# Second-layer output tiles placed behind three products instead of two in the group loop of a fused MLP and adapter kernel

## The reference

```python
attn_out = softmax(x Wq (x Wk)^T * scale) (x Wv) @ Wp + bp
cms_out  = gelu(attn_out @ cW1 + cb1) @ cW2 + cb2 + one_hot(codes)
modifier = gelu(concat[attn_out, cms_out] @ mW1 + mb1) @ mW2 + mb2
x        = clip(x + cms_out + modifier, 0, 1)
h        = x + gelu(x @ W_down[stream] + b_down) @ W_up[stream] + b_up
out      = layernorm(h) * ln_w[stream] + ln_b[stream]
```

## Time and profile before

| | |
|---|---|
| median of 3 runs | 1073.81 us (1073.79 to 1074.4) |
| time of the profiled execution | 1073.88 us |
| its span | 1072.0 us |
| PE busy | 1063.9 us (99%), 4753 instructions |
| PEld busy | 881.3 us (82%) |
| DVE busy | 598.1 us (56%) |
| POOL busy | 542.0 us (51%) |
| ACT busy | 452.6 us (42%) |
| granted clock of PE | full in all 40 slices |

### The profile page before, as it was taken

How to read it: one execution, slowest core, us unless ns; L and a number is a source line. 1 busy time by engine, 2 the same in 40 slices (tenths; PEclk the granted TensorE clock), 3 DMA queues, 4 the chain that set the end, 5 groups by cost and what they waited for, 6 DMA issues and landing times.

```text
span 1072.0 us, 13168 instructions
## 1 busy us (share of the span) xinstructions
PE 1063.9 (99%) x4753; PEld 881.3 (82%) x4753; DVE 598.1 (56%) x838; ACT 452.6 (42%) x868; POOL 542.0 (51%) x555
## 2 busy tenths in 40 slices
PE   9999999999999999999999999999999999999997
PEld 8888888888888888888888888888878888888886
DVE  4735344395565565566774445555885445545568
ACT  4624336353343333333454333343644433342664
POOL 0501154542243232332798667666997667753406
PEclk9999999999999999999999999999999999999999
DMA  7401010101223213112132221223934221123834
GB/s 276 139 1 40 1 40 20 40 0 45 74 73 123 100 73 108 36 34 65 60 109 84 84 84 66 83 84 140 354 121 167 84 79 55 64 69 147 294 79 157
DMA packets 62063, 100.50 MB, mean 94 GB/s; under 512 B 5680, under 2 KB 35376, under 8 KB 61488
## 3 DMA queue, kind: packets, MB, share of 16 engines
q1 hardware_dynamic: 61424, 98.62, 26.8%
q10 hardware_dynamic: 576, 1.05, 0.3%
HBM read 77.63 MB, written 22.02 MB: 93 GB/s over the span
## 4 chain that ended last, share of the span: by engine, by line
PE 92%; DVE 4%; POOL 3%; issue 1%; ACT 1%; DVEq 0%; ACTq 0%; POOLq 0%
PE bank L736 30%; PE bank L738 30%; PE bank L737 30%; DVE z L1522 1%; DVE stats L1516 1%; PE bank L793 1%; DVE c_T_f L1321 1%; POOL c_B_lo L568 1%; POOL left_c L568 0%; POOL left_x L568 0%; PE bank L762 0%; POOL c_T_lo L568 0%; DVE H_lo L1369 0%; DVE mean_var L1518 0%; POOL W_lo L568 0%
## 5 line engine op out<-in xcount | busy, mean ns | idle before, releaser
L1398 DVE TENSOR_TENSOR acc<-bank,acc 128x512 f32<-128x512 f32 x224 | 151.4, 687 | 88.9 <-PE bank L738 88.2
L736 PE MATMUL bank<-H_hi,W_hi 128*128 128x512 f32 x512 | 199.3, 389 | 0.7 <-POOL W_lo L568 0.7
L737 PE MATMUL bank<-H_lo,W_hi 128*128 128x512 f32 x512 | 199.2, 389 | 0.0
L738 PE MATMUL bank<-H_hi,W_lo 128*128 128x512 f32 x512 | 199.2, 389 | 0.0
L568 POOL TENSOR_TENSOR left_x<-rawX,left_x 128x256 fp32r<-128x256 f32 x144 | 126.8, 881 | 99.7 <-ACT left_x L992 99.7
L992 ACT ACTIVATE left_x<-rawX 128x256 fp32r<-128x256 f32 x144 | 58.0, 410 | 167.9 <-DMA rawX<-mW_dram 86.2
L1381 DVE TENSOR_TENSOR u_t<-bank,s_t 128x512 f32<-128x512 f32 x64 | 44.2, 690 | 131.8 <-PE bank L738 125.1
L736 PEld LDWEIGHTS bank<-H_hi,W_hi 128*128 128x128 f32 x512 | 96.1, 188 | 21.0 <-POOL W_lo L568 1.2
L738 PEld LDWEIGHTS bank<-H_hi,W_lo 128*128 128x128 f32 x512 | 96.1, 188 | 20.1
L737 PEld LDWEIGHTS bank<-H_lo,W_hi 128*128 128x128 f32 x512 | 96.1, 188 | 19.9
L736 PE MATMUL bank<-x_T_hi,left_x 128*128 128x512 f32 x256 | 99.6, 389 | 0.0
(11 more groups left out here) (195 smaller groups left out, 2309.0 us busy)
## 6 DMA issues: line engine op xcount, KB each, us to landing
rawX<-mW_dram SPq DMA_DIRECT2D x16, 512.0 KB, 3.9
rawC<-mW_dram SPq DMA_DIRECT2D x16, 512.0 KB, 5.0
W_raw<-mW_dram SPq DMA_DIRECT2D x16, 512.0 KB, 3.7
xT_raw<-xT_dram SPq DMA_DIRECT2D x4, 1024.0 KB, 8.3
x_raw<-x_dram SPq DMA_DIRECT2D x4, 1024.0 KB, 6.1
rawX<-cW_dram SPq DMA_DIRECT2D x8, 512.0 KB, 3.8
W_raw<-cW_dram SPq DMA_DIRECT2D x8, 512.0 KB, 3.7
out_dram<-z SPq DMA_DIRECT2D x16, 256.0 KB, 2.0
```

The lines of the kernel that those rows point to most:

```text
L736: pe.matmul(tile, sh, mh, start=first_one and n == 0, stop=False, skip_group_check=joined_group)
L737: pe.matmul(tile, sh, ml, start=False, stop=False, skip_group_check=joined_group)
L738: last = pe.matmul(tile, sl, mh, start=False, stop=last_one and n == len(terms) - 1, skip_group_check=joined_group)
L1398: op = dve.tensor_tensor(dst, src, dst, ALU.add)
```

## The change

A function `first_of` gives the number of products that PE issues before the first four output tiles: 2 in groups 17 and 24, 3 in all others. Group 16 leaves the loop before it is used, and group 0 has no output tiles, so the order changes in groups 1 to 15, 18 to 23 and 25 to 31, 28 groups in all. In these product 2 now stands ahead of `out_tiles(g - 1, 0)`, and was behind it. The second four output tiles stay behind product 4. No instruction is added or removed on any engine, and the orders of DVE, ACT, POOL and SP are the same.

```diff
+            def first_of(g):
+                return 2 if g in (MOD0 + 1, 24) else 3
...
                 else:
-                    for i in order_of(g)[g == 0:2]:
+                    for i in order_of(g)[g == 0:first_of(g)]:
                         product_part(g, i, sources)
                 if g > 0:
                     out_tiles(g - 1, 0)
-                for i in order_of(g)[2:5]:
+                for i in order_of(g)[first_of(g):5]:
                     product_part(g, i, sources)
                 if g > 0:
                     out_tiles(g - 1, 1)
```

## The result

| | median | lowest to highest | runs |
|---|---|---|---|
| before | 1074.06 us | 1073.57 to 1074.74 | 9 |
| changed | 1076.92 us | 1076.3 to 1078.45 | 9 |

The ratio is 1.003, with a 95% interval from 1.0019 to 1.004: slower by 2.86 us. That is 0.27%; the interval begins at 0.19%, just under the 0.2% that the prediction called the limit of a measurement. The forecast was 1074.5 us, no change, with a range up to 1075.8. The profiled execution took 1076.82 us, 2.94 more than that of before.

A forecast was written before the change was run, and what follows sets the result against it. PE was taken as the bound, so only its waits count. Group 1's 1.76 us less group 25's 1.03 gives +0.73 on 1073.88, 1074.61; with the median 0.07 below, 1074.5 us, range 1073.3 to 1075.8.

The forecast's parts named there:

- What bounds the kernel: Whole kernel: PE, busy 1063.9 of 1072.0 us and 92% of the chain; only its waits can change the time.
- The cms groups 2 to 14 and the modifier groups: Product 2's operands are ready with at least 1.34 us to spare in cms groups, 4.55 in modifier group 21: cost nothing.
- Group 1, 1.76 us: Group 1: PE newly waits for T1 from DVE, 1.63 us late plus 0.13 for slower steps.
- Group 25, 1.03 us gained: Group 25: product 2 covers PE's wait for `W_lo`, recovering 0.90 us and 0.13 for slower steps.
- The output tiles, later by a product: Group 15: DVE's last additions come 1.36 us later, delaying ACT and POOL; taken as 0, at worst 1.16 us.
- the upper bound of 1.16: Group 15's worst case: all 1.36 us of delay arrive, less 0.33 spare, plus 0.13 for slower steps.
- Rival 2: POOL's queue of groups 15 to 17 arrives late at 558.37: 1075.2 us, or 1075.7 with all the delay; chance 0.14.
- Rival 1: The clock falls once in group 1 during PE's new idle time: 1076.4 us, over 0.2% slower; chance 0.04.
- Rivals 3 and 4: Group 25's wait stays, 1075.6 us, chance 0.05; group 1 costs nothing, T1 being ready earlier, 1072.8 us, chance 0.03.

The follow-up runs named there:

- `not1`: The changed kernel with group 1 back at two products ahead of the output tiles: 1075.24 us, ratio 1.0013 against the kernel before.
- `t1_first`: The changed kernel with DVE writing the low half of T1 in group 1 ahead of two rows of its own: 1075.27 us, ratio 1.0012.
- `only25`: The kernel before with three products ahead of the output tiles in group 25 alone: 1073.65 us, ratio 0.9995.
- `sp_swap`: The changed kernel with SP's load of the next adapter piece in group 16 moved behind the eight cms saves: 1077.16 us, ratio 1.0029.
- `saves_first`: The changed kernel with SP issuing group 16's first four cms saves ahead of the loads of `rawX` and the piece: 1077.65 us, ratio 1.0029, four runs.
- `only15`: The kernel before with three products ahead of the output tiles in group 15 alone: 1076.85 us, ratio 1.0026.
- `only25_26`: The kernel before with three products ahead of the output tiles in groups 25 and 26: 1072.98 us, ratio 0.999.

## Why the prediction was right or wrong

The forecast of 1074.5 us was 2.4 us too low, and the time lies outside the range. Two terms of its sum came true; a third, put at nothing, did not.

**What bounds the kernel:** right. PE's share of the chain is 95% after, and each loss over 0.2 us was PE waiting for another engine's row.

**The cms groups 2 to 14 and the modifier groups:** right. None of those that moved lost more than 0.02 us. Group 24, which did not move, lost 0.15 us more than before; no run was made on it.

**Group 1, 1.76 us:** right, 1.81 lost, at 222.83 where 222.59 was forecast (the kernel began 0.15 us later). `not1` took it away and `t1_first` showed that two DVE rows made it.

**Group 25, 1.03 us gained:** right in size, 1.04. The sum took it as belonging to one place. Group 26's move may have been needed too (`only25`, not shown for certain); the change had both.

**"The output tiles, later by a product", group 15, taken as 0:** this is the step that failed. It cost 2.0 to 2.8 us between medians, beyond the upper bound of 1.16 as well. Its own reason was right: POOL's rows met less of DVE, and were only 0.7 us late. But the 0.49 us for which POOL waited for ACT before 538.56 were counted as spare, and I did not ask what ACT waited for. In the kernel before, ACT waited 0.23 us for the save of `cms_kept`. So that wait had no room at all. Between DVE's last addition and this save lies SP's queue, where a load stood ahead that was itself late (mending that alone gave back 0.5 of 1.8 us, `sp_swap`), and the DMA engines, where the load of `rawX` held the saves (`saves_first`). The step left both out. It also weighed the overlap with DVE for the two `rawX` rows only. The prediction's own sentence, that the delay could move POOL onto another of DVE's rows and block it anew, is what happened at 542.80, on the row right behind them, and made that row 0.75 us longer. Its upper bound took 1.36 us of delay to arrive as 1.36 at most, but ACT's row came 2.3 us later against PE.

One reading ahead of the step was wrong too: the prediction took the list of waits to mean that PE waited nowhere else inside the stream. The kernel before lost 0.13 us in group 16, at a matmul at 541.93, too little for the list. DVE's row on `c_T_lo` had ended 0.15 us ahead of it (540.01 + 1.77 = 541.78), which is about as far as PE started behind its releaser in group 1. So this stretch seems to have had no room in a second place as well.

**Rival 2** named the right work, POOL's rows of groups 15 to 17, and the wrong place: 558.37. The loss came at 544.34 first. Its own place did show, in `only15` and `saves_first`.

**Rival 1**, the clock, fell. PE was idle for 1.55 us before 222.83, and the granted clock of the windows around it, the third value from the end (the DMA share and GB/s follow), is 1.00:

```profile
216.00:224.00 8.00, 6.45 (x29) 5.03 (x28) 7.87 (x11) 7.58 (x12) 0.03 (x1) 1.00 0.00 0
224.00:230.00 6.00, 6.00 (x28) 4.94 (x28) 5.51 (x7) 1.67 (x3) 5.41 (x4) 1.00 0.00 0
```

PE stayed at its upper level of 2.4 GHz. The Trainium skill, TensorE: Matmul & The Clock Gate, section "A second HAM failure mode: psum-queue depth-cycling", would have allowed for a fall; this single idle time did not make one. The rival's price, 1.86 us, is not shown by a row either: in the kernel before the granted clock is 1.00 in each of the first six microseconds, so the slow transposes of the earlier trace rows are no measure of the lower level.

**Rivals 3 and 4** fell: `W_lo` was ready 1.76 us before its output tile, and T1 was no earlier than its row said.

## What to carry to other kernels

Before an operation of a full stream is moved, read at each place what its waits have to spare, and follow every queue behind what is made later, the DMA issue queue too: an engine that waits for another is not spare time until it is known what that other one waited for. The repeated groups of a steady stage took the new order for nothing; the first group, and the last before a change of stage, paid. A wait that goes can come back one group later when what was late hangs on a transfer, and may do so in some executions only, so a gain is to be followed for as many groups as the pattern repeats, and over more than one execution.

## What the runs showed of the hardware

- Four saves of 256 KB landed at most 3.1 us after the last tile's sum with the load of `rawX` (512 KB) issued behind them, 3.4 with it issued 3.3 us ahead of that sum (kernel before), and 4.7 to 5.2 us with it issued 2.3 us ahead.
- One load of 1024 KB took 5.7, 5.9 and 7.1 us from issue to landing in three executions (kernel before, `only25_26`, `only25`).
- One DVE instruction with two SBUF inputs (128x512) took 0.68 us alone and up to 2.65 beside POOL. A POOL row of 128x256 on `left_c` took 0.74 us when it started 0.20 us before a DVE row with two SBUF inputs (`sp_swap`), and 1.49 when it started 0.31 us behind one (changed kernel).
- An idle time of PE of 1.55 us between dense matmuls left the granted clock at 1.00.
- The loss of several short waits, each under half a microsecond, doesn't show in a list of waits, because the matmul rows overlap: `sp_swap` lost 1.77 us in groups 16 and 17 with none listed.
